# Moving VectorE's length chain between the row maxima in a six-attention stack, with masks and tests on GpSimd

## Chip, cores and metric

The kernel runs on one core of one Trainium2 chip. The metric is the device time of one execution in microseconds. TensorE is called PE here, ScalarE ACT, VectorE DVE, GpSimd POOL and SyncE SP, as in the profile.

## What is computed

A batch of 32 items, each 128 tokens by 256 features in f32, goes through six attentions of 16 heads one after the other. Five have heads of 16 features ("narrow"), the fifth (attention 4) has heads of 64 ("wide"). Two feed-forwards stand behind attentions 1 and 3, and each of the eight parts ends in a residual sum and a layer norm. Cut to what matters here:

```python
mask0 = 1.0 - all(x == 0)                      # per token; mask1 the same on x1
def _mha(x, kv, Wq, Wk, Wv, m, causal):        # attentions 0 and 1
    Q, K, V = (x @ Wq) * m, (kv @ Wk) * m, (kv @ Wv) * m
    energy = Q @ K.T
    lengths = sum(energy[:, :, 0, :] != 0)     # per head, from query row 0
    energy = where(cols >= lengths or (causal and cols > row), -inf, energy)
    return softmax(energy / sqrt(dk)) @ V * m
def mha(q, kv, ...):                           # attentions 2 to 5
    Q, K, V = q @ wq + bq, kv @ wk + bk, kv @ wv + bv
    return softmax(mask(Q @ K.T / sqrt(dk))) @ V @ wo + bo
x = layer_norm(x + attention) * g + b
```

A softmax row sums to 1, so a bias on V adds `bv @ wo` to every output row.

## The kernel before

All weights stay in SBUF. The 32 items go in four rounds of eight. A round has six stages, one for each attention, and a stage has eight slots, one for each item: slot `n` has attention `att(n)` and item `batch(n)` (lines 99 to 112), so there are 192 slots. Stages are called 0 to 5 after their attention; the first two, which find a length, are 0 and 1.

The work of one item is spread over some five slots. Each step has an offset in slots in the table `NARROW` (line 115) or `BROAD` (line 118). `make_orders` (line 125) adds the offset to the slot's number, and sorts. What comes out is one fixed list of steps for each engine, and each engine walks down its list: a step that waits holds up everything behind it on that engine. A step on PE that fills a PSUM tile (`tile`, line 132) has its reader, on ACT or DVE, 0.03 of a slot later. `AFTER_SCORES` is the distance between a score step on PE and the two things read from scores, `max` on DVE and `exp` on ACT.

The steps of a narrow item, in its own order: `XT` (transpose x), `K` and `Q` (projections; ACT evicts K and Q, GpSimd's `keys` expands K), `L` (product of query row 0 with the keys, for the length; GpSimd's `q0` prepares the query), `V`, the score step S, `MT` (the negated row maxima turned by PE, and folded by DVE into Q), the turned score step T, `exp`, `PV` (probabilities times V), `E1` (turned back; DVE divides), and for attentions 2 to 5 `E2` and `E3` (output projection); then `LN` and `LN end`. A feed-forward adds `XT`, `F1`, `F2` and a norm.

Scores have two PSUM buffers, SC0 and SC1, for the halves h = 0 and 1 of the heads. One PE step `ST` does S of one item and T of the item before the last at the same time, in different buffers. There are two of them in a slot: the first writes S into SC0 and T into SC1, the second S into SC1 and T into SC0. So before S is written, the `exp` that reads the T written there last must be done (`free_scores`, lines 510 to 518):

```python
                before = BANK_BEFORE[(part, u)]
                if before[0] == "S":
                    pe.wait_ge(maxima, done("max", before[1]))
                else:
                    pe.wait_ge(probs, done("exp", before[1]))
```

`MT` waits for the second maximum of its slot (line 708). Small tiles go round in a ring of four (`TILES`, line 46), and each waits until the fourth before it has been read. `L` on DVE (lines 1043 to 1067) is a chain of seven instructions, each waiting for the one before; it ends in the keys, which the next S needs. The token mask of attention 1's context is made by `token mask` on POOL (line 1213), `SM` on PE (line 620) and a product on DVE (line 1009).

Of the kernel before, what the change touches and what calls it, by code (L numbers as in the profile page):

```python
# [35 lines left out]
P = 128  # L36
# [86 lines left out]


def make_orders():
# [10 lines left out]
    def norm(at, what, n):  # L136
        put("DVE", at, "LN", what, n)
        put("POOL", at + 0.01, "rstd", what, n)
        put("DVE", at + LN_END, "LN end", what, n)

    steps = {}
    for n in range(SLOTS):
# [32 lines left out]
        tile(n + o["V"], "ACT" if a in (0, 1) else "DVE", "V", n, 0)  # L175
# [21 lines left out]
        if a == 0:  # L197
            put("DVE", n + o["LN"] + LN_END + 0.01, "seen1", b)
# [21 lines left out]
ON_TILES = {"XT", "CT", "SM", "K", "Q", "V", "L", "MT", "PV", "PVW", "E1", "E2", "E3", "F1", "F2", "TP"}  # L220
# [17 lines left out]
def score_bank_users():  # L238
# [32 lines left out]
    "norm_end": [it[1:] for it in pick("DVE", {"LN end"})],  # L271
    "add": [it[1:] for it in pick("POOL", {"add"})],
# [7 lines left out]
assert INDEX["norm"] == INDEX["rstd"] == INDEX["norm_end"] and INDEX["length"] == INDEX["q0"]  # L280
# [41 lines left out]
def build(nc, x, ctx_in, mask_ss, mask_bs, weights, col_bias, row_vec, consts, out):  # L322
    with ExitStack() as stack:
# [6 lines left out]
        def sem(name):  # L330
# [23 lines left out]
        O, OnT, Y, xc = ring(1, "O", [P, D]), ring(1, "OnT", [P, D]), ring(1, "Y", [P, D]), ring(2, "xc", [P, D])  # L354
# [86 lines left out]
        def _(sp):  # L441
# [31 lines left out]
            for kind, b in ORDER["SP"]:  # L473
# [4 lines left out]
                elif kind == "c" and b >= 2:  # L478
                    sp.wait_ge(tile_full, done("tile", ("CT", b - 2)))
# [6 lines left out]
                elif kind == "store":  # L486
                    sp.wait_ge(normed, done("norm", ("att", slot(b, 5))))
# [6 lines left out]
        def _(pe):  # L494
# [109 lines left out]
            for it in ORDER["PE"]:  # L604
# [3 lines left out]
                if kind == "XT":  # L608
# [302 lines left out]
        def _(dve):  # L911
# [58 lines left out]
            for it in ORDER["DVE"]:  # L970
# [344 lines left out]
```

## Time and profile before

| | |
|---|---|
| three runs, median (lowest to highest) | 2756.04 us (2753.00 to 2758.52) |
| the profiled execution, its own time | 2755.75 us |
| its span in the profile | 2753.6 us |
| mean granted clock of TensorE | 0.952 of full speed |
| busy: PE, PE weight loads | 2519.1 us (91%), 2094.6 us (76%) |
| busy: DVE, ACT, POOL | 1600.2 us (58%), 1376.2 us (50%), 827.1 us (30%) |
| chain that ended last, by engine | PE 72%, DVE 11%, issue 7%, POOL 5%, ACT 4% |

The span is the time between the first and the last instruction; the execution's own time has 2.2 us more around it. A busy share is a mean over stages that differ, so the slots have to be looked at stage by stage. The start of each `MT` on PE, one for each narrow slot, is used below to mark slots.

### The profile page before, as it was taken

The page shows a single profiled execution, that of the slowest core. Times are in us where ns is not written, and L with a number is a line of the kernel's source. Part 1 is how long each engine was busy: PE and PEld are TensorE (multiplying, and loading weights), DVE is VectorE, ACT ScalarE, POOL GpSimd, SP SyncE. Part 2 cuts the span into 40 slices and gives each one's busy share as a digit, 9 for nine tenths or more (in the row PEclk, how much of TensorE's full clock was granted, in tenths as well). Part 3 has the DMA queues.
Part 4 walks back from the last instruction along what each step waited for, and adds up shares of the span by engine and source line. Part 5 has one row for each costly group of instructions (what it writes and reads, how often), then busy time and mean ns, then how long its engine had stood idle before and what let it go on. Part 6 is the DMA issues. An engine that isn't in the chain of part 4 may idle for free.

```text
span 2753.6 us, 70667 instructions
## 1 busy us (share of the span) xinstructions
PE 2519.1 (91%) x28737; PEld 2094.6 (76%) x28737; DVE 1600.2 (58%) x3528; ACT 1376.2 (50%) x3364; POOL 827.1 (30%) x1412
## 2 busy tenths in 40 slices
PE   6879999999887999999988899999998889999998
PEld 5667887887766788787766688888786668888876
DVE  4677753445766775344576676544466676644446
ACT  2344565554444456555544456555454445655544
POOL 1234322223233432222323343222232344312222
PEclk8889999999998999999999899999999889999999
DMA  7000000000100000000000000000000000000000
GB/s 245 7 2 2 2 2 1 1 1 10 36 6 2 2 2 2 1 1 2 21 26 4 2 2 2 2 1 1 1 27 23 2 2 2 2 1 1 1 1 17
DMA packets 23778, 32.28 MB, mean 12 GB/s; under 512 B 2305, under 2 KB 22177, under 8 KB 23329
## 3 DMA queue, kind: packets, MB, share of 16 engines
q1 hardware_dynamic: 23456, 27.78, 3.1%
q8 instruction: 229, 3.75, 0.6%
q14 instruction: 93, 0.75, 0.1%
HBM read 23.57 MB, written 4.19 MB: 10 GB/s over the span
## 4 chain that ended last, share of the span: by engine, by line
PE 72%; DVE 11%; issue 7%; POOL 5%; ACT 4%; POOLq 0%; DMA 0%; DVEq 0%; SPq 0%; ACTq 0%
PE M L522 40%; PE SC L685 12%; PE M L528 7%; PE M L721 4%; DVE nmax L1084 3%; POOL Kx L1202 3%; PE M L738 2%; PE SC L584 2%; PE SC L703 2%; PE SC L559 2%; ACT Pr L862 2%; DVE Kx L1063 1%; POOL Y L1228 1%; DVE stats L1151 1%; DVE len_row L1057 1%
## 5 line engine op out<-in xcount | busy, mean ns | idle before, releaser
L1234 POOL TENSOR_TENSOR rstd<-rstd,half 128x1 f32<-128x1 f32 x256 | 184.5, 721 | 1202.6 <-DVE rstd L1155 1201.7
L522 PE MATMUL M<-XT,W 128*128 128x128 f32 x4096 | 540.8, 287 | 2.5 <-ACT H L904 1.5
L522 PEld LDWEIGHTS M<-XT,W 128*128 128x128 f32 x4096 | 519.0, 203 | 20.0 <-issue 2.7
L1084 DVE TENSOR_REDUCE nmax<-SC 128x8 f32<-128x1024 f32 x320 | 389.6, 1217 | 92.0 <-PE SC L685 92.0
L1202 POOL TENSOR_SCALAR Kx<-K,own,k_ones 128x128 f32<-128x128 f32 x640 | 279.6, 451 | 498.7 <-ACT K L815 357.1
L685 PEld LDWEIGHTS SC<-Kx,Qx 32*128 32x128 f32 x5120 | 341.6, 200 | 91.9 <-issue 87.7
L685 PE MATMUL SC<-Qx,Kx 32*128 32x128 f32 x5120 | 398.4, 297 | 0.9 <-DVE Qx L1023 0.9
L685 PE MATMUL SC<-Kx,Qx 32*128 32x128 f32 x5120 | 394.7, 296 | 1.5 <-DVE nmax L1084 1.5
L685 PEld LDWEIGHTS SC<-Qx,Kx 32*128 32x128 f32 x5120 | 333.8, 198 | 3.3 <-issue 1.3
L871 ACT ACTIVATE Pr<-SC 128x1024 f32<-128x1024 f32 x256 | 261.6, 1022 | 69.7 <-PE SC L584 44.3
L841 ACT ACTIVATE Qx<-M,q_bias,q_scale 128x128 f32<-128x128 f32 x640 | 241.8, 474 | 23.4 <-PE M L522 23.4
L862 ACT ACTIVATE Pr<-SC,nmax_w 128x128 f32<-128x128 f32 x512 | 139.0, 383 | 183.3 <-DVE nmax_w L1087 158.1
L1128 DVE TENSOR_TENSOR Y<-M,X 128x256 f32<-128x256 f32 x128 | 54.1, 423 | 271.2 <-PE M L522 271.2
L522 PE MATMUL M<-CT,W 128*128 128x128 f32 x1536 | 207.5, 286 | 0.0
L522 PEld LDWEIGHTS M<-CT,W 128*128 128x128 f32 x1536 | 189.0, 197 | 14.7 <-issue 7.6
L815 ACT ACTIVATE K<-M 128x256 f32<-128x256 f32 x64 | 24.5, 383 | 336.5 <-PE M L522 336.5
L522 PE MATMUL M<-W,CT 128*128 128x512 f32 (+1 forms) x512 | 191.6, 497 | 0.0
L818 ACT ACTIVATE K<-M,CB 128x128 f32<-128x128 f32 x192 | 60.2, 366 | 260.8 <-PE M L522 260.8
L721 PE MATMUL M<-Pr,V 128*32 128x128 f32 x5120 | 173.8, 277 | 0.0
L1252 POOL TENSOR_TENSOR Pr<-Pr,wrec 128x1024 f32<-128x1024 f32 x64 | 121.3, 1895 | 156.7 <-DVE wrec L1099 156.7
L528 PE MATMUL M<-ident,nmax 128*128 128x128 f32 x160 | 48.4, 302 | 130.0 <-DVE nmax L1084 129.9
L798 ACT ACTIVATE XT<-M 128x256 f32<-128x256 f32 x256 | 97.8, 390 | 137.3 <-PE M L528 137.2
(127 smaller groups left out, 4460.3 us busy)
## 6 DMA issues: line engine op xcount, KB each, us to landing
X<-x SPq DMA_DIRECT2D x32, 128.0 KB, 2.1
c_in<-ctx_in SPq DMA_DIRECT2D x32, 128.0 KB, 2.1
out<-X SPq DMA_DIRECT2D x32, 128.0 KB, 1.7
RV<-row_vec SPq DMA_DIRECT2D x1, 2304.0 KB, 12.1
W<-w_k SPq DMA_DIRECT2D x5, 256.0 KB, 9.0
W<-w_q SPq DMA_DIRECT2D x5, 256.0 KB, 12.1
W<-w_v SPq DMA_DIRECT2D x5, 256.0 KB, 7.8
W<-w_f SPq DMA_DIRECT2D x1, 1024.0 KB, 8.9
```

The source lines that it names most:

```text
L522: last = pe.matmul(dst, a, b, start=(k == 0), stop=(k == len(lhsTs) - 1))
L528: last = pe.transpose(dst[:, i * P:(i + 1) * P], src[:, i * P:(i + 1) * P], ident[:, :])
L685: filled[at] = pe.matmul(dst, lhsT, rhs, start=(starting and i == 0), stop=(i == len(line) - 1), skip_group_check=True)
L721: last = pe.matmul(tile_of(it)[32 * t:32 * t + 32, b * P:(b + 1) * P], on_ring(V16, "narrow", n)[:, 4 * b + t, :], p[:, at:at + P], start= ...
L798: act.activation(XT[i % len(XT)][:, :], tile_of(it)[:, 0:D], ACT.Copy).then_inc(tile_act, 1)
L841: last = act.activation(q[:, half_of, c * P:(c + 1) * P], tile_of(it)[:, c * P:(c + 1) * P], ACT.Identity, bias=q_bias[:, which, c, half_o ...
L862: last = act.activation(p[:, i * P:(i + 1) * P], SC[u % 2][:, i * P:(i + 1) * P], ACT.Exp, bias=nm[:, i:i + 1])
L871: last = act.activation(p[:, :], SC[u % 2][:, :], ACT.Exp)
L1084: dve.tensor_reduce(nm, SC[h][:, :].rearrange("p (g c t) -> p g c t", c=KC, t=P), AX_X, ALU.max, negate=True).then_inc(maxima, 1)
L1202: last = pool.tensor_scalar(kx[:, half_of, c * P:(c + 1) * P], k[:, c * P:(c + 1) * P], own[:, half_of:half_of + 1], k_ones[:, half_of, c: ...
L1234: pool.tensor_tensor(r[:, :], r[:, :], half[:, :], ALU.pow).then_inc(rstd_done, 1)
L1252: pool.tensor_tensor(p, p, on_ring(wrec, "wide", u)[:, :].unsqueeze(2).to_broadcast([P, HU, P]), ALU.mult).then_inc(wide_norm, 1)
```

## The change

The steps of the narrow slots get other offsets. `L` moves up on all engines, on DVE to between the two maxima, and the norm `LN` goes behind the second. `AFTER_SCORES` grows from 0.12 to 0.19, for `max` and `exp` alike, in all narrow stages. ACT makes a small column of the first query (`q_col`) before it evicts Q, so that `q0` on POOL need not wait for Q. `L` loses one instruction. The two tests for empty rows go to POOL, only their maxima stay on DVE. The context's mask becomes a product on POOL in place (`context`), a second transpose on PE (`CM`) and an eviction on ACT; `SM` is gone. V's biases are folded once into the rows of the output biases (`VT`, `VB`, in slots 9 to 12 of the first round); V is then only copied, in attention 2 by ACT instead of DVE. The sum `Y` and the statistics `mv` have two buffers instead of one. `by_pool` returns False always, so the branches for a norm on ACT and POOL emit nothing.

```diff
-NARROW = dict(XT=-1.20, SM=-1.25, K=-0.92, Q=-0.86, L=-0.42, V=0.30, CT=0.40, MT=0.86, PV=2.66, E1=3.20, E2=3.54,
-              E3=3.74, XF=4.40, F1=4.62, F2={1: 4.90, 3: 5.10},
-              seen0=-1.15, keys=-0.88, q0=-0.78, mask_row=-0.30, residual=3.30, LN=3.40, SF=0.14)
+NARROW = dict(XT=-1.14, CM=-1.10, CT=-1.92, K=-0.94, Q=-0.88, L=-0.64, V=0.28, MT=0.93, PV=2.62, E1=3.20, E2=3.54,
+              E3=3.72, XF=4.24, F1=4.40, F2={1: 4.66, 3: 4.95}, seen0=-1.0, context=-1.75, keys=-0.80, q0=-0.86,
+              mask_row=-0.30, residual=3.32, LN=3.84)
...
+V_BIAS_AT = {2: 9.32, 3: 10.32, 4: 11.32, 5: 12.32}
 S_STEP, T_STEP = (0.0, 0.5), (1.5, 2.0)
-AFTER_PE, AFTER_SCORES = 0.03, 0.12
-LN_END = 0.25
+AFTER_PE, AFTER_SCORES = 0.03, 0.19
+LN_END = 0.22
...
+def by_pool(norm):
+    return False
...
-        tile(n + o["V"], "ACT" if a in (0, 1) else "DVE", "V", n, 0)
+        tile(n + o["V"], "ACT" if a in (0, 1, 2) else "DVE", "V", n, 0)
...
+                elif kind == "CM":
+                    b = it[1]
+                    pe.wait_ge(cm_done, done("batch", b))
+                    turn(tile_of(it), c_in[b % 2], KC).then_inc(tile_full, 1)
...
+                    if a in MASKED_BY_LENGTH:
+
+                        i = AT["q0"][n]
+                        if i >= 2:
+                            act.wait_ge(q0_done, i - 1)
+                        act.activation(q_col[i % 2][:, :], chunks(tile_of(it)[:, 0:D])[:, :, 0], ACT.Copy,
+                                       scale=DK ** -0.5).then_inc(q_first, 1)
...
-                    dve.tensor_tensor(on_ring(V16, "narrow", n)[:, :, 0:DK],
-                                      tile_of(it)[:, 0:D].rearrange("p (h d) -> p h d", d=DK),
-                                      row(f"v{att(n)}").rearrange("p (h d) -> p h d", d=DK),
-                                      ALU.add).then_inc(tile_dve, 1)
+                    dve.tensor_copy(on_ring(V16, "narrow", n)[:, :, 0:DK],
+                                    tile_of(it)[:, 0:D].rearrange("p (h d) -> p h d", d=DK)).then_inc(tile_dve, 1)
...
+                    dve.tensor_tensor(r, tile_of(it)[:, 0:D], r, ALU.add).then_inc(tile_dve, 1)
...
-                    dve.reciprocal(crec[:, :], cnt[:, :]).then_inc(len_rec, 1)
-                    dve.wait_ge(len_rec, done("length", n))
-
-                    dve.scalar_tensor_tensor(out=lval[:, :], in0=crec[:, :], scalar=-BIG, in1=cnt[:, :], op0=ALU.mult,
-                                             op1=ALU.mult).then_inc(len_val, 1)
+                    dve.reciprocal(lval[:, :], cnt[:, :]).then_inc(len_val, 1)
...
+                    pool.wait_ge(q_first, done("q0", n))
...
+                    pool.tensor_scalar(c_in[b % 2][:, :], c_in[b % 2][:, :], seen1[lane(b)][:, 0:1], None,
+                                       ALU.mult).then_inc(cm_done, 1)
```

**ACT, a slot of stage 5.** `K` and `Qx` are the evictions of K and Q, `Pr<-SC` is an exp, `OnT` evicts E2, `OT` evicts PV. Before, and then with the change:

```order
L818 ACTIVATE K<-M,CB 128x128 x2
L871 ACTIVATE Pr<-SC 128x1024
L841 ACTIVATE Qx<-M,q_bias,q_scale 128x128 x4
L897 ACTIVATE OnT<-M 128x256
L871 ACTIVATE Pr<-SC 128x1024
L885 ACTIVATE OT<-M 128x512
L798 ACTIVATE XT<-M 128x256
```

```order
L869 ACTIVATE K<-M,CB 128x128 x2
L899 ACTIVATE Qx<-M,q_bias,q_scale 128x128 x4
L929 ACTIVATE Pr<-SC 128x1024
L948 ACTIVATE OnT<-M 128x256
L942 ACTIVATE OT<-M 128x512
L929 ACTIVATE Pr<-SC 128x1024
L835 ACTIVATE XT<-M 128x256
```

The first exp has moved from ahead of the eviction of Q to behind it, the second from ahead of the eviction of PV to behind it. The order on PE is the same in this stage. The two moves are in every narrow stage.

**DVE, a slot of stage 0.** `nmax<-SC` is a maximum, `ne` to `Kx` is the length chain, `stats` to `xc` the norm. Both pieces begin with the division behind E1, which follows the first maximum. Before, and then with the change:

```order
L1117 SCALAR_TENSOR_TENSOR O<-M,seen_2,rec 128x256
L1151 BN_STATS stats<-Y 128x6
L1153 BN_AGGR mv<-stats 128x2
L1155 TENSOR_SCALAR rstd<-mv 128x1
L1158 SCALAR_TENSOR_TENSOR xc<-Y,mv,RV 128x256
L1046 TENSOR_SCALAR ne<-M,spare_row 128x128
L1049 TENSOR_REDUCE cnt<-ne 128x1
L1051 RECIPROCAL crec<-cnt 128x1
L1054 SCALAR_TENSOR_TENSOR lval<-crec,cnt 128x1
L1057 TENSOR_SCALAR len_row<-iota,cnt,lval 128x128
L1063 SCALAR_TENSOR_TENSOR Kx<-len_row,spare,Kx 128x256 x2
L1084 TENSOR_REDUCE nmax<-SC 128x4x2
```

```order
L1174 SCALAR_TENSOR_TENSOR O<-M,seen_1,rec 128x256
L1107 TENSOR_SCALAR ne<-M,spare_row 128x128
L1110 TENSOR_REDUCE cnt<-ne 128x1
L1112 RECIPROCAL lval<-cnt 128x1
L1114 TENSOR_SCALAR len_row<-iota,cnt,lval 128x128
L1120 SCALAR_TENSOR_TENSOR Kx<-len_row,spare,Kx 128x256 x2
L1141 TENSOR_REDUCE nmax<-SC 128x4x2
L1207 BN_STATS stats<-Y 128x6
L1216 BN_AGGR mv<-stats 128x2
L1218 TENSOR_SCALAR rstd<-mv 128x1
L1223 SCALAR_TENSOR_TENSOR xc<-Y,mv,RV 128x256
```

The norm no longer stands ahead of the chain and the second maximum; it follows them.

## Rows read from the trace of the kernel before

**Rows 1.** Windows: second round by stage; us, busy (instructions) per engine, clock, DMA
```profile
703.38:802.91 99.53, 83.98 (x1110) 65.58 (x1111) 68.36 (x176) 42.45 (x91) 27.90 (x64) 0.95 0.07 20
802.91:908.53 105.62, 85.73 (x1076) 72.22 (x1077) 70.97 (x171) 42.95 (x92) 39.30 (x80) 0.84 0.01 2
908.53:991.69 83.16, 83.16 (x1134) 66.39 (x1133) 59.40 (x128) 43.68 (x98) 36.04 (x64) 1.00 0.01 2
991.69:1026.67 34.98, 34.98 (x540) 29.26 (x539) 26.06 (x57) 20.86 (x44) 12.58 (x24) 1.00 0.01 3
1026.67:1085.89 59.22, 59.22 (x716) 53.15 (x715) 33.45 (x78) 38.63 (x81) 16.27 (x28) 1.00 0.01 2
...
1328.40:1379.10 50.70, 48.72 (x768) 40.88 (x768) 36.08 (x74) 30.96 (x66) 17.28 (x35) 1.00 0.10 28
```
**Rows 2.** Waits of TensorE: who for whom, us in total, times, longest
```profile
PE M L528 <- DVE nmax L1084: 129.9, 71, 3.5
PE M L625 <- POOL seen_diag L1219: 30.0, 32, 1.5
```
**Rows 3.** Timeline, TensorE then VectorE, one slot of stage 0 (start, us, engine, line)
```profile
764.01 0.30 PE L528 MATMUL M<-ident,nmax 128*128 128x128 f32 x1 [2.30 <-DVE nmax L1084]
764.15 0.59 PE L559 MATMUL SC<-causal_b,ident_b 128*128 128x512 bf16 x2
766.22 1.95 PE L522 MATMUL M<-XT,W 128*128 128x128 f32 x16
775.94 0.39 PE L528 MATMUL M<-ident,nmax 128*128 128x128 f32 x1 [2.35 <-DVE nmax L1084]
...
772.30 0.34 DVE L1046 TENSOR_SCALAR ne<-M,spare_row 128x128 f32<-128x128 f32 x1
774.58 1.21 DVE L1084 TENSOR_REDUCE nmax<-SC 128x8 f32<-128x1024 f32 x1
```
**Rows 4.** Timeline, TensorE then ScalarE, one slot of stage 5
```profile
676.56 0.27 PE L528 MATMUL M<-ident,nmax 128*128 128x128 f32 x1
677.86 1.16 PE L522 MATMUL M<-CT,W 128*128 128x128 f32 x8
678.86 1.06 PE L522 MATMUL M<-XT,W 128*128 128x128 f32 x8
679.75 0.60 PE L528 MATMUL M<-ident,OT 128*128 128x128 f32 x4
681.15 0.38 PE L685 MATMUL SC<-Kx,Qx 32*128 32x128 f32 x2
682.62 1.08 PE L721 MATMUL M<-Pr,V 128*32 128x128 f32 x32
684.82 0.27 PE L528 MATMUL M<-ident,nmax 128*128 128x128 f32 x1
...
679.57 1.02 ACT L871 ACTIVATE Pr<-SC 128x1024 f32<-128x1024 f32 x1
680.48 1.51 ACT L841 ACTIVATE Qx<-M,q_bias,q_scale 128x128 f32<-128x128 f32 x4
683.01 1.02 ACT L871 ACTIVATE Pr<-SC 128x1024 f32<-128x1024 f32 x1
683.91 0.60 ACT L885 ACTIVATE OT<-M 128x512 f32<-128x512 f32 x1
```
**Rows 5.** Timeline of TensorE: two waits and the matmuls behind the first
```profile
644.85 0.33 PE L528 MATMUL M<-ident,nmax 128*128 128x128 f32 x1 [1.45 <-DVE nmax L1084]
646.19 1.99 PE L522 MATMUL M<-CT,W 128*128 128x128 f32 x8
...
703.38 0.30 PE L528 MATMUL M<-ident,nmax 128*128 128x128 f32 x1 [1.39 <-DVE nmax L1084]
```
**Rows 6.** Groups by line: count, busy, mean ns, idle before (ScalarE)
```profile
L798 ACT ACTIVATE XT<-M 128x256 f32<-128x256 f32 x256 | 97.8, 390 | 137.3 <-PE M L528 137.2
L869 ACT ACTIVATE Pr<-SC,key_bias 128x1024 f32<-128x1024 f32 x64 | 71.5, 1117 | 0.1
```

More of the change, by code:

```diff
@@ L138, in norm @@
         put("POOL", at + 0.01, "rstd", what, n)
-        put("DVE", at + LN_END, "LN end", what, n)
+        if by_pool((what, n)):
+            put("ACT", at + 0.12, "normalise", what, n)
+            put("POOL", at + 0.18, "affine", what, n)
+        else:
+            put("DVE", at + LN_END, "LN end", what, n)
     steps = {}
@@ L164, in make_orders @@
         if a == 0:
-            put("DVE", n + o["seen0"], "seen0", b)
+            put("DVE", n + o["seen0"], "largest0", b)
+            put("POOL", n + o["seen0"] + 0.08, "seen0", b)
+        if a == 1:
             tile(n + o["CT"], "ACT", "CT", b)
-        if a == 1:
-            put("POOL", n + o["SM"] - 0.20, "token mask", n)
-            tile(n + o["SM"], "DVE", "SM", n)
+            put("POOL", n + o["context"], "context", b)
+            tile(n + o["CM"], "ACT", "CM", b)
         if a == 3:
@@ L208, in make_orders @@
         put("PE", at, "ST", parts.get("S"), parts.get("T"))
+    for a, at in V_BIAS_AT.items():
+        if a == WIDE:
+            put("DVE", at, "v bias wide", a)
+        else:
+            tile(at, "DVE", "VT", a)
+        tile(at + 0.40, "DVE", "VB", a)
     for b in range(BATCH):
@@ L271 @@
     "norm_end": [it[1:] for it in pick("DVE", {"LN end"})],
+    "affine": [it[1:] for it in pick("POOL", {"affine"})],
     "add": [it[1:] for it in pick("POOL", {"add"})],
@@ L279 @@
 BANK_BEFORE = score_bank_users()
-assert INDEX["norm"] == INDEX["rstd"] == INDEX["norm_end"] and INDEX["length"] == INDEX["q0"]
+assert INDEX["norm"] == INDEX["rstd"] and INDEX["norm_end"] == [key for key in INDEX["norm"] if not by_pool(key)]
+assert INDEX["affine"] == [it[1:] for it in pick("ACT", {"normalise"})] and INDEX["length"] == INDEX["q0"]
 assert INDEX["narrow"] == INDEX["keys"] == INDEX["e1"]
@@ L613, in _ @@
                         what, a = XT_AFTER[j]
-                        pe.wait_ge(normed, done("norm", (what, slot(b, a))))
+                        if by_pool((what, slot(b, a))):
+                            pe.wait_ge(normed_pool, done("affine", (what, slot(b, a))))
+                        else:
+                            pe.wait_ge(normed, done("norm_end", (what, slot(b, a))))
                     turn(tile_of(it), X[lane(b)], KC).then_inc(tile_full, 1)
@@ L883, in _ @@
                         act.wait_ge(tile_full, done("tile", ("E1", before[1]) if before[0] == "PV" else ("E3", before[1] // 2)))
-                    if kind == "PV":
-                        last = act.activation(o[:, :], tile_of(it)[:, :], ACT.Copy)
-                    else:
-                        for t in range(4):
-                            last = act.activation(o[:, t * P:(t + 1) * P], tile_of(it)[:, t * P:(t + 1) * P],
-                                                  ACT.Identity, bias=bias("v4", 4 * (it[1] % 2) + t))
-                    last.then_inc(tile_act, 1)
+                    act.activation(o[:, :], tile_of(it)[:, :], ACT.Copy).then_inc(tile_act, 1)
                 elif kind == "E2":
@@ L967, in _, with free_sum @@
             dve.wait_ge(masks_turned, 1)
+            dve.tensor_scalar(iota[:, :], iota[:, :], -1.0 / BIG, None, ALU.mult)
             dve.tensor_copy(key_bias[:, :], M[TILES - 1][:, 0:BATCH]).then_inc(ready_dve, 1)
+            def free_sum(key):
+                i = AT["norm"][key]
+                if i >= len(Y):
+                    before = INDEX["norm"][i - len(Y)]
+                    if by_pool(before):
+                        once(normalised, done("affine", before))
+                    else:
+                        once(centred, done("norm_end", before))
             for it in ORDER["DVE"]:
```

182 lines of the change are left out of this document (120 added, 62 removed).

## Prediction

> **What bounds the kernel now.** I began with the busy shares: TensorE 91%, nothing else over 58%. That is a mean, so the second view is the round cut by stages [rows 1]. The second round's stages 0 and 1 take 99.53 and 105.62 us with PE busy 83.98 and 85.73; in stages 2 and 3 PE is busy for the whole of 83.16 + 34.98 + 59.22 us, and in the last row, six slots of stage 5, for 48.72 of 50.70. So there are two regimes. Where a length is found, PE waits; elsewhere it is full, and only less PE work or a new wait can change the time. The third view is who PE waits for [rows 2]: 129.9 us for the row maxima, 30.0 us for the token mask.
>
> The timeline of one slot of stage 0 shows why [rows 3]. MT starts at 764.01 and again at 775.94, a slot of 11.93 us, and the second MT waited 2.35. The chain ahead of it is VectorE's: the length chain from 772.30 to the maximum at 774.58 (2.28), then the maximum, 1.21. The scores for that maximum were ready long before; it stood behind norm and chain in VectorE's list. In stage 1 the mask's wait comes on top. The granted clock there is 0.84, in stage 0 it is 0.95, elsewhere 1.00 [rows 1]: waiting makes PE slow as well.
>
> Now the full regime [rows 4]. In stage 5 a slot is 684.82 - 676.56 = 8.26 us with no wait. ACT does exp at 679.57, then evicts Q (680.48 to 681.99); PE writes the second score step at 681.15, just 0.56 after that exp ended at 680.59. The second exp ends at 684.03, PV's eviction follows it. The score buffers are thus freed barely in time. Keep this in view.
>
> **The change, part by part.**
>
> *What VectorE gains in stages 0 and 1.* The chain starts after E1 instead of after the norm. It also loses one small instruction, and two tests go to POOL, which is idle 70% of the span. The maximum then finds both its scores and an idle engine: it no longer sets MT, except where a feed-forward's F2, now just ahead of the second maximum in VectorE's list, holds it.
>
> *What ACT's new order costs in every narrow slot.* The first exp now stands behind Q's eviction, the second behind PV's. PE may not write S before that exp has read the old T. I lay the rows end to end for stage 5, from the first score step at 0. Score step 1.10 (676.76, by its offset behind MT, to 677.86). K and Q on PE 2.06 (677.86 to the end of Q at 679.92), so 3.16. Hop to ACT 0.05, eviction of Q 1.51: 4.72. Exp 1.02, less 0.10 by which ACT's instructions overlap: 5.64. Hop back 0.15 (VectorE's maximum ends at 775.79, MT starts at 775.94 [rows 3]): 5.79. PE would have been there at 4.39, the distance from 676.76 to 681.15: a wait of 1.4. Second step 1.10, O's transposes 0.37 (PV starts at 682.62, which is 1.47 after the step), PV 1.08: 8.34. Hop 0.05, eviction of PV 0.60, exp 0.92, hop 0.15: 10.06. **The slot becomes 10.06 us instead of 8.26.** Six slots of it a round: +10.8 us.
>
> *Stage 2* has mask matmuls in its steps, 2.07 each (764.15 to 766.22 [rows 3]), and K and Q 1.95. The same sum gives 11.9 us. Four of its eight slots also carry stage 1's feed-forward. There x's transpose is evicted behind that exp too (0.39 [rows 6]) and F1 stands ahead of the score step; F2 stands ahead of the maximum. The sum with 0.95 for F1 and for F2 (half of the 16 matmuls of [rows 3]) and 0.5 for F2's sum on VectorE (an estimate: under half of a maximum, which reads four times its columns) is 13.15, 13.15, 14.1 and 14.45. Total 47.6 + 54.9 = 102.5 against 83.16: +19.3.
>
> *Stage 3*: its exp takes 1.12 [rows 6], and each step has a row mask more, an estimated 0.1; hence 10.5, with 1 us more in the first two for stage 2's last masks: 43.4 against 34.98 [rows 1], +8.4. Its four last slots carry the large feed-forward, and PE has enough of its own to cover the exps, but F1 waits for the transpose behind the exp: reached at 4.9, free at 6.2, +1.3 each, +5.2.
>
> *Stage 0* by the same chain: 2.07 + 1.95 + 0.05 + q_col 0.25 + 1.50 + 0.92 + 0.15 + 2.07 + 1.08 + 0.05 + 0.60 + 0.92 + 0.15 = 11.76, against 11.93 at full clock today. So the freed maximum is worth almost nothing: the exps take its place as what PE waits for. Six such slots and two of 11.2: 93.0. q_col is not in the trace. It lies between 0 and the 0.39 of a whole 256-column eviction [rows 6]; I take 0.25, since its two columns leave only the fixed part. The Trainium skill (ScalarE: Activation LUTs, "What ACT_TABLE_LOAD costs") states 186 ns plus 0.833 ns a column for an ACTIVATE with immediate operands. By it q_col is 0.19, and the whole sum 3 us lower.
>
> *Stage 1*: two slots of 11.05, two of 10.1, and four with F1 and F2, 12.7 each, where F1 waits for the transpose and MT for F2 and the maximum: 93.0.
>
> *The rest.* V's bias prelude: four small products and sums once, in slots full of waits, +4 us. CM and CT: four transposes for one small matmul, in the slots above. PVW's evictions become one instead of four, and V is copied instead of added: both off PE's path. The wide stage keeps its own table; I take it as unchanged.
>
> **Sum.** Per round at full clock: +10.8 + 19.3 + 8.4 + 5.2 = +43.7 in the full stages. Stages 0 and 1 go from 205.15 to 186.0, -19.1. Net +24.6, in four rounds +98, with the prelude +102: 2858.
>
> *The clock.* Half speed holds for twice the missing share of the clock: 10 us in stage 0 and 34 in stage 1 [rows 1]. At PE's share of 0.83 this cost 44 x 0.5 x 0.83 = 18 us a round, and the 186.0 above has none of it. The waits get shorter (1.2 to 1.4 instead of 1.85 to 2.36) but there are two a slot. What a wait of this size does, the trace answers both ways [rows 5]: behind 1.45 at 644.85 eight matmuls took 1.99 instead of the 1.16 at 677.86 [rows 4], half speed; behind 1.39 at 703.38 nothing slowed. Bounds 0 and 18; I take half, 9 a round, +36 in all.
>
> The execution profiled took 2755.75, 0.3 under the median of 2756.04, so the sum holds against either: **2894 us**.
>
> **Rivals.**
>
> 1. *The clock does not fall at all* behind waits this short: 2858. For it: four slots with 1.39 and full speed. Against: 644.85.
>
> 2. *The clock falls in every stage that now waits.* The full stages (then 272 us a round) would get stage 0's or stage 1's share of half speed. At 0.95 that is 272 x 0.05 x 0.83 = 11 us a round, at 0.84 it is 36. With 18 in stages 0 and 1: 2858 + 4 x (18 + 11) = 2974, or 3074 at worst. For it: 17% of a slot idle, like stage 0 now; two short waits lie near transposes and 32-row score matmuls. Against: never seen below 1.45. The Trainium skill (TensorE: Matmul & The Clock Gate, "Part 4: PE-mode transpose") says that transposes don't count as work for the clock as other matmuls do. By it this rival's 2974 would be the time, since XT, O and MT stand beside the waits; the slots of 1.39, which have XT right ahead of the wait, speak against it.
>
> 3. *Faster: the exps stay hidden and PE runs full in stages 0 and 1.* Then these 205.15 us shrink to PE's own 169.7 less 18 for the clock, 152: -53 a round, and 2756 - 4 x 53 = 2544. The point that decides is whether Q's eviction plus exp (2.43) fits beside E1 and V on PE (679.75 to 681.15, 1.40). By [rows 4] it does not, in any narrow stage. Smaller gains would need that wait at under a third of my value.
>
> 4. *No change*: the losses of stages 2, 3 and 5 are about 19 a round instead of 43.7. Needs the same.
>
> **How the numbers follow.** Forecast 0.55, rival 1 0.17, rival 2 0.20, rival 3 and smaller gains 0.06, no change 0.02. A measurement of this kernel tells about 0.2% (5.5 us) from nothing. So faster 0.06, same 0.02, slower 0.92. The range: from 2858 down by the bound of q_col and hops that are 0.1 shorter (some 35 us) to 2820, up to rival 2 and a little of its worse half, 2990. That leaves out rivals 3 and 4 and the far end of 2.
>
> **What would show it.** In stages 2, 3 and 5 PE's busy share falls from 100% to about 83%, and PE's waits are for ACT's `Pr`, in two groups, at score steps, some 1.4 and 0.3 us. A slot of stage 5 takes 10.1 us from MT to MT. PE's wait for `nmax` falls from 129.9 to under 40 us, mostly where F2 is; the wait for the token mask is gone. In stage 0 a slot is 11.8, in stage 1's last half 12.7. It is wrong if PE stays at 100% in stage 5, or if stages 0 and 1 fall under 170 us a round.

## The result, and the profile after

The changed kernel takes 2781.31 us (median of 4 runs, 2777.55 to 2785.78) against 2757.28 for the kernel before on the same chip (2753.0 to 2758.53). The ratio is 1.0091, 95% interval 1.0071 to 1.011. So it is slower by 24 us, or 0.9%: little, but clear of the noise. 138 us were forecast, and the time lies under the low end of the range (2820). The profiled execution took 2782.93.

The page of the changed kernel, busy time of TensorE and the chain that ended last:

```profile
PE 2462.5 (89%) x28803; PEld 2019.6 (73%) x28803; DVE 1569.2 (56%) x3346; ACT 1365.4 (49%) x3300; POOL 870.3 (31%) x1476
PE 74%; ACT 16%; issue 5%; DVE 4%; ACTq 0%; POOL 0%; DMA 0%; SPq 0%; POOLq 0%; DVEq 0%
```

PE is *less* busy than before (2519.1 us), though it has slightly more matmuls (28803, before 28737): fewer of them ran slowly, the mean granted clock is 0.990 instead of 0.952. ACT's share of the chain went from 4% to 16%, DVE's from 11% to 4%. Who PE waits for (total, times, longest):

```profile
PE SC L722 <- ACT Pr L929: 69.2, 92, 1.6
PE SC L583 <- ACT Pr L929: 68.8, 87, 1.2
PE M L552 <- DVE nmax L1141: 59.1, 52, 1.6
PE M L546 <- ACT XT L835: 50.6, 45, 1.4
```

The waits for maximum and mask [rows 2] fell from 129.9 to 59.1 and from 30.0 to nothing, and some 138 us of waits for exps took their place. The 50.6 us in the last row are for the transposes that the first product of a feed-forward, F1, reads; their evictions now stand behind an exp on ACT. Now the windows of the second round by stage, cut at the same `MT`s as [rows 1]: 0, 1, 2, first half of 3, second half of 3, the wide stage, stage 5.

```profile
707.62:798.90 91.28, 79.31 (x1102) 59.84 (x1101) 67.71 (x154) 40.67 (x94) 32.67 (x74) 1.00 0.06 18
798.90:890.15 91.25, 75.09 (x1100) 62.65 (x1098) 70.00 (x152) 48.19 (x116) 44.13 (x84) 1.00 0.03 9
890.15:991.62 101.47, 85.30 (x1128) 64.99 (x1129) 53.54 (x123) 45.69 (x104) 36.09 (x64) 1.00 0.01 2
991.62:1033.32 41.70, 35.52 (x540) 29.25 (x539) 26.26 (x57) 21.20 (x45) 12.57 (x24) 1.00 0.01 2
1033.32:1100.39 67.07, 61.93 (x733) 54.55 (x731) 32.95 (x78) 42.16 (x87) 17.14 (x28) 1.00 0.01 2
1100.39:1325.40 225.01, 217.22 (x1762) 183.18 (x1760) 99.82 (x188) 109.28 (x310) 55.55 (x54) 0.98 0.00 1
1325.40:1393.86 68.46, 58.20 (x839) 48.62 (x840) 39.84 (x78) 33.40 (x72) 19.34 (x40) 0.95 0.06 17
```

Stages 0 and 1 gained 8.3 and 14.4 us. Stage 2 lost 18.3, stage 3 lost 6.7 and 7.9. The clock column reads 1.00 in all of them. The wide stage fell from 234.96 to 225.01, which no step of the prediction had. Some 2 us of this are only the mark: the second half of stage 3 now holds 16 more of the products `M<-CT,W` than before (716 matmuls then, 733 now), and the wide stage 16 fewer. Stage 5 lost 10.0, and there the clock reads 0.95 (0.97 before).

The timeline of one slot of stage 5, TensorE and then ScalarE, the counterpart of [rows 4]:

```profile
1354.41 0.27 PE L552 MATMUL M<-ident,nmax 128*128 128x128 f32 x1
...
1360.59 0.38 PE L722 MATMUL SC<-Kx,Qx 32*128 32x128 f32 x2 [1.21 <-ACT Pr L929]
...
1364.26 0.27 PE L552 MATMUL M<-ident,nmax 128*128 128x128 f32 x1
1364.77 0.38 PE L722 MATMUL SC<-Kx,Qx 32*128 32x128 f32 x2 [0.24 <-ACT Pr L929]
...
1358.12 1.50 ACT L899 ACTIVATE Qx<-M,q_bias,q_scale 128x128 f32<-128x128 f32 x4 [0.27 <-PE M L546]
1359.50 1.03 ACT L929 ACTIVATE Pr<-SC 128x1024 f32<-128x1024 f32 x1
1363.21 0.60 ACT L942 ACTIVATE OT<-M 128x512 f32<-128x512 f32 x1 [0.66 <-PE M L758]
1363.70 1.02 ACT L929 ACTIVATE Pr<-SC 128x1024 f32<-128x1024 f32 x1
```

This is the picture that the prediction drew: the exp starts as Q's eviction ends (1359.50), ends at 1360.53, and PE writes scores at 1360.59 after 1.21 us of waiting; the second exp costs 0.24. The slot is 9.85 us (forecast 10.06, before 8.26).

### The profile page after: what moved, and what is told of

It is laid out like the page before. It is cut to its first block, busy times and chain, and to the rows that moved or that the text cites. A ratio compares the mean times of both kernels' runs of the same rounds, so it can differ in the third digit from the quotient of the medians.

```text
span 2781.1 us, 70879 instructions
## 1 busy us (share of the span) xinstructions
PE 2462.5 (89%) x28803; PEld 2019.6 (73%) x28803; DVE 1569.2 (56%) x3346; ACT 1365.4 (49%) x3300; POOL 870.3 (31%) x1476
## 4 chain that ended last, share of the span: by engine, by line
PE 74%; ACT 16%; issue 5%; DVE 4%; ACTq 0%; POOL 0%; DMA 0%; SPq 0%; POOLq 0%; DVEq 0%
PE M L546 40%; PE SC L722 14%; ACT Pr L929 7%; PE M L552 6%; ACT Qx L899 6%; PE M L758 6%; PE SC L583 3%; PE SC L608 2%; PE M L775 2%; PE SC L740 2%; DVE nmax L1141 2%; ACT Pr L927 1%; ACT Pr L920 1%; ACT XT L835 1%; DVE nmax_w L1144 1%
## 5 line engine op out<-in xcount | busy, mean ns | idle before, releaser
L546 PE MATMUL M<-XT,W 128*128 128x128 f32 x4096 | 523.5, 280 | 50.6 <-ACT XT L835 50.6
L546 PEld LDWEIGHTS M<-XT,W 128*128 128x128 f32 x4096 | 495.4, 195 | 76.1 <-ACT XT L835 56.9
L722 PEld LDWEIGHTS SC<-Kx,Qx 32*128 32x128 f32 x5120 | 320.9, 189 | 141.9 <-ACT Pr L929 77.3
L722 PE MATMUL SC<-Kx,Qx 32*128 32x128 f32 x5120 | 370.5, 283 | 58.6 <-ACT Pr L929 57.5
L722 PE MATMUL SC<-Qx,Kx 32*128 32x128 f32 x5120 | 372.1, 283 | 0.9 <-DVE Qx L1087 0.9
L722 PEld LDWEIGHTS SC<-Qx,Kx 32*128 32x128 f32 x5120 | 311.1, 186 | 3.1 <-ACT Pr L929 1.1
L942 ACT ACTIVATE OT<-M 128x512 f32<-128x512 f32 x224 | 134.3, 599 | 315.9 <-PE M L758 215.7
L758 PEld LDWEIGHTS M<-Pr,V 128*32 128x32 f32 x5120 | 130.0, 109 | 33.2 <-issue 27.9
L546 PE MATMUL M<-W,H 128*128 128x256 f32 x640 | 152.0, 384 | 0.0
```

The costliest lines, as they stand in the source:

```text
L546: last = pe.matmul(dst, a, b, start=(k == 0), stop=(k == len(lhsTs) - 1))
L722: filled[at] = pe.matmul(dst, lhsT, rhs, start=(starting and i == 0), stop=(i == len(line) - 1), skip_group_check=True)
L758: last = pe.matmul(tile_of(it)[32 * t:32 * t + 32, b * P:(b + 1) * P], on_ring(V16, "narrow", n)[:, 4 * b + t, :], p[:, at:at + P], start= ...
L942: act.activation(o[:, :], tile_of(it)[:, :], ACT.Copy).then_inc(tile_act, 1)
```

## The experiments

All times are whole-kernel medians, taken on several chips, on which the kernel before took 2754.7 to 2760.0; ratios are against the kernel before, run on the same chip beside them. The table has the second round by stage in us, from `MT` to `MT` in the timelines.

| kernel | 0 | 1 | 2 | 3, first | 3, second | wide | 5 | time | ratio (95%) |
|---|---|---|---|---|---|---|---|---|---|
| before | 99.5 | 105.6 | 83.2 | 35.0 | 59.2 | 234.9 | 58.5 | 2757 | 1 |
| changed | 91.3 | 91.3 | 101.5 | 41.7 | 67.1 | 225.0 | 68.5 | 2781.3 | 1.0091 (1.0071 to 1.011) |
| e1, exps early | 82.0 | 88.0 | 93.2 | 35.0 | 68.1 | 224.0 | 58.8 | 2637.8 | 0.9551 (0.9535 to 0.9568) |
| e2, before with exps late | 108.6 | 98.7 | 96.5 | 41.7 | 68.8 | 227.7 | 68.9 | 2899.7 | 1.0494 (1.0473 to 1.0516) |
| e3, old FF places | 91.3 | 83.8 | 95.6 | 41.7 | 78.9 | 225.1 | 66.9 | 2778.3 | 1.0058 (1.0043 to 1.0073) |
| e4, PVW in four | 91.3 | 91.2 | 101.5 | 41.7 | 67.1 | 225.1 | 68.5 | 2783.4 | 1.0083 (1.0066 to 1.01) |
| e5, e1 with F1, F2 later | 81.9 | 83.6 | 84.8 | 35.0 | 66.7 | 221.9 | 57.2 | 2582.1 | 0.9375 (0.9358 to 0.9393) |
| e6, first exp early | 86.3 | 88.3 | 94.4 | 36.4 | 65.9 | 225.1 | 61.0 | 2668.0 | 0.9686 (0.9669 to 0.9702) |
| e7, e1 with old chain | 112.0 | 120.7 | 93.2 | 35.0 | 68.0 | 222.9 | 58.4 | 2889.8 | 1.0489 (1.0474 to 1.0505) |
| e8, e1 with F2 later | 81.9 | 83.6 | 87.1 | 35.0 | 68.0 | 224.2 | 55.6 | 2598.5 | 0.9426 (0.9408 to 0.9444) |
| e9, e7 with early maxima | 108.6 | 115.1 | 87.1 | 35.0 | 68.0 | 221.3 | 58.3 | 2827.2 | 1.0262 (1.0245 to 1.028) |
| e10, before with new chain | 89.4 | 84.0 | 83.2 | 35.0 | 59.2 | 235.8 | 56.8 | 2623.9 | 0.9525 (0.9511 to 0.9539) |
| e11, e1 with old FF places | 81.9 | 81.3 | 82.3 | 35.0 | 63.7 | 224.2 | 57.2 | 2556.5 | 0.9282 (0.9266 to 0.9297) |
| e12, e10 with PV at 2.62 | 89.4 | 84.0 | 83.2 | 35.0 | 59.2 | 226.6 | 60.1 | 2596.5 | 0.9428 (0.9412 to 0.9445) |

**The exps alone, both ways.** e1 puts only the exps back; e2 moves only the exps in the kernel before.

```diff
 # e1, in the changed kernel
-            put("ACT", n + T_STEP[h] + AFTER_SCORES, "exp", u)
+            put("ACT", n + T_STEP[h] + 0.12, "exp", u)
 # e2, in the kernel before
-            put("ACT", n + T_STEP[h] + AFTER_SCORES, "exp", u)
+            put("ACT", n + T_STEP[h] + 0.20, "exp", u)
```

> The changed kernel with one number undone: the exps of the narrow attentions stand 0.12 of a slot behind their scores on ACT again (ahead of Q's and PV's evictions), the maxima stay at 0.19. Theory (the late exps are the whole loss; the moved length chain is a gain): stages 2, 3 and 5 get back the 43 us a round that they lost, and stages 0 and 1 lose their waits for Pr too, some 10 us a round more: 2781 - 4 x 53 = 2570 us, at least under 2625. Rival (exps early delay q_col and with it the length chain, so that the maximum is late again in stages 0 and 1, +10 us a round or more there): 2640 to 2680. Rival (the loss is from another edit, such as the feed-forward's new place): about 2780.

> The kernel before with that one move alone: the exps 0.20 of a slot behind the scores on ACT, behind Q's and PV's evictions; all else as before. Theory: +40 us a round in stages 2, 3 and 5 and little in 0 and 1, whose slots are set by VectorE there: 2757 + 160 = 2917 us, more if the two waits add up in stages 0 and 1. Rival (exps are hidden, other edits cost the time): 2757 to 2770.

Measured: 143.5 us gained by e1 against the changed kernel, 139.7 lost by e2 against the kernel before on the same chip (2760.0). The move costs nearly the same from either side, and so it does in three places: about 9 us in stage 0, 7 in the first half of 3 and 10 in stage 5. Elsewhere the two differ (8 and 13 us in stage 2, -1 and +10 in the second half of 3, 1 and -7 in the wide stage, 3 and -7 in stage 1), so that the totals agree so well is partly chance. In e1 the narrow exps are gone from PE's waits; in e2 they stand there with 84.3, 73.1 and 49.4 us, beside 136.8 for the maximum that e2 left in place. In stage 1 e2 even got shorter (105.6 to 98.7): PE was busy for 75.8 us there instead of 85.7 with the same matmuls, at a clock of 0.95 instead of 0.84, and its wait for the token mask fell from 6.9 us to 0.2. Why the clock held better is open.

**Which exp.** e6 moves only the first back.

```diff
-            put("ACT", n + T_STEP[h] + AFTER_SCORES, "exp", u)
+            put("ACT", n + T_STEP[h] + (AFTER_SCORES, 0.12)[h], "exp", u)
```

> The changed kernel with only the first exp of a slot (half 0, behind the first score step) put back ahead of Q's eviction; the second stays behind PV's. By the rows laid end to end, a slot of stage 5 is then 7.1 + 0.05 + 0.60 + 0.92 + 0.15 = 8.8 us, against 8.26 with both early and 9.85 with both late; stage 0 is 10.75. Theory (each exp has its own wait, Q's eviction the dearer): some 11 us a round more than with both early: 2680 us. Rival (one late exp is enough to lose it all): 2750 to 2781.

2668.0: the exp behind Q's eviction costs 113 us, the one behind PV's the other 30. Of the 143.5 these are 79% and 21%; of the waits in a slot of stage 5, 1.21 and 0.24, they would be 83% and 17%. The second exp alone late was tried, the first alone late was not.

**Feed-forward places.** e3 undoes them in the changed kernel, e8 and e5 move part of them in e1, e11 undoes them all in e1.

```diff
-              E3=3.72, XF=4.24, F1=4.40, F2={1: 4.66, 3: 4.95}, ...
+              E3=3.72, XF=4.40, F1=4.62, F2={1: 4.90, 3: 5.10}, ...   (e3 and e11)
+              E3=3.72, XF=4.24, F1=4.40, F2={1: 4.72, 3: 4.95}, ...   (e8)
+              E3=3.72, XF=4.24, F1=4.52, F2={1: 4.72, 3: 4.95}, ...   (e5)
```

> The changed kernel with the feed-forwards' old offsets (XF 4.40, F1 4.62, F2 4.90 and 5.10). The wide stage took 235 us a round before and takes 225 now. Theory A (the gain there is F1's eviction, which now stands ahead of the wide exp instead of behind it): it returns to about 235, while the feed-forward slots of stages 1 to 3 lose their waits for F1's transpose and for F2, some 3 + 5 + 5 us: 2775 to 2790 us. Theory B (the gain comes from PVW's single eviction): the wide stage stays at 225, and the total falls to 2730 or so.

> e1_exp_early with F2 of attention 1 at 4.72 alone, so that on VectorE it follows the second maximum. Theory (MT waits 1.4 to 1.5 us in eight slots a round because the maximum stands behind F2): 2638 - 4 x 10 = 2598 us. Rival (the wait only moves, PE has to wait at MT or F2 anyway): 2630 to 2638.

> e1_exp_early with the feed-forwards moved: F1 at 4.52, behind the second score step, so that it no longer stands ahead of it waiting for the transpose, and F2 of attention 1 at 4.72, behind the second maximum on VectorE. Theory (F1's wait for the transpose and the maximum behind F2 cost stages 1 and 2 some 12 us a round, stage 3 some 5 to 8): 2638 - 4 x 18 = 2565 us. Rival (F1's eviction comes too late for the wide stage's transposes and its 4.7 us wait returns): 2590 to 2620.

> The changed kernel with the exps at 0.12 and all feed-forward steps (XF, F1, F2) where they were before. What is left of the change against e10_chain_alone is then the work taken off VectorE (mask as a product on GpSimd, tests on GpSimd, one instruction fewer in the chain), q_col, and V's biases. Theory (these help: e10 still waits 71 us on TensorE for GpSimd's `q0`, which q_col starts a micro-second earlier): 2570 to 2595, some 40 us under e10's 2624, and the waits for `q` fall under 10 us. Rival (they are neutral, and e5_ff_later's 2582 came from its own places of F1 and F2): 2610 to 2640.

With the exps late the places are a draw: e3 gains 13 us a round in stages 1 and 2 and gives 12 back in the second half of stage 3. With the exps early they are a plain loss: e8 gets 39 us back by F2 behind the maximum alone (34 by the ratios), e5 another 14 to 16 by F1, and e11, with all at their old places, takes 2556.5, 81 under e1 and the best kernel here. What a place is worth depends on which wait is open beside it.

e3's second half of stage 3 also shows the clock falling behind a wait. Timeline of TensorE there, a long wait and the matmuls behind it:

```profile
1035.81 0.39 PE L722 MATMUL SC<-mask_row,ones_b 1*128 1x512 bf16 x2 [2.47 <-ACT Pr L927]
1037.02 1.74 PE L546 MATMUL M<-CT,W 128*128 128x128 f32 x8
...
1043.13 1.05 PE L546 MATMUL M<-XT,W 128*128 128x128 f32 x8
```

Eight matmuls take 1.74, half speed, just behind the wait, and 1.05 a few us later. Its window, 1033 to 1112, has a clock of 0.94.

**PVW's eviction**, split in four again in the changed kernel.

```diff
-                    act.activation(o[:, :], tile_of(it)[:, :], ACT.Copy).then_inc(tile_act, 1)
+                    if kind == "PV":
+                        last = act.activation(o[:, :], tile_of(it)[:, :], ACT.Copy)
+                    else:
+                        for t in range(4):
+                            last = act.activation(o[:, t * P:(t + 1) * P], tile_of(it)[:, t * P:(t + 1) * P], ACT.Copy)
+                    last.then_inc(tile_act, 1)
```

> The changed kernel with PVW's eviction in four instructions again (without the bias, which stays folded), so 0.5 us more on ACT, 64 times. Theory A (the wide stage's gain is F1's place): no change within 0.2%, 2781. Theory B (it is PVW's eviction): the wide stage goes back to 235 us a round, 2820.

2783.4 against 2781.3, and no stage moved: nothing, so this is not where the wide stage's 10 us came from. The trace names another place. The timeline of TensorE and then ScalarE in the wide stage of the kernel before:

```profile
1114.68 1.12 PE L528 MATMUL M<-ident,Pr 128*128 128x128 f32 x4 [4.75 <-ACT H L904]
...
1112.20 1.28 ACT L904 ACT_TABLE_LOAD   x1
1113.49 2.17 ACT L904 ACTIVATE H<-M,CB 128x128 f32<-128x128 f32 x8
1115.50 0.65 ACT L885 ACTIVATE OT<-M 128x512 f32<-128x512 f32 x1
```

The same in the changed kernel:

```profile
1124.14 0.65 PE L552 MATMUL M<-ident,Pr 128*128 128x128 f32 x4 [1.13 <-ACT OT L942]
...
1111.96 1.28 ACT L955 ACT_TABLE_LOAD   x1
1114.26 1.14 ACT L955 ACTIVATE H<-M,CB 128x128 f32<-128x128 f32 x4 [1.02 <-PE M L546]
...
1116.27 1.14 ACT L955 ACTIVATE H<-M,CB 128x128 f32<-128x128 f32 x4 [0.59 <-PE M L546]
```

And the window of 20 us at this place, of the kernel before and then of the changed one:

```profile
1110.00:1130.00 20.00, 15.32 (x105) 12.84 (x106) 6.00 (x11) 12.71 (x37) 2.58 (x2) 0.83 0.00 1
```

```profile
1110.00:1130.00 20.00, 18.87 (x179) 16.59 (x178) 8.22 (x16) 13.23 (x34) 6.03 (x5) 1.00 0.00 1
```

Before, PE stood 4.75 us behind one table load and eight evictions of the large feed-forward in a row, and ran slowly behind that (clock 0.83 in this window). After, the load is over before PE's product comes, and the evictions stand in two pieces of four. e10 (below), which has the old table but for chain and norm, still has the 4.75; e11, with the *old* feed-forward places, has 1.05. So it is not F1's place. PV at 2.62 instead of 2.66 was left as a suspect: it puts PV's eviction between the two pieces. e12 tried it alone, in e10.

```diff
-... V=0.30, CT=0.40, MT=0.86, PV=2.66, ...
+... V=0.30, CT=0.40, MT=0.86, PV=2.62, ...
```

> The kernel of e10_chain_alone with the offset of PV at 2.62 instead of 2.66, as the change has it. On ScalarE this puts PV's eviction between the two halves of the eviction of the large feed-forward's H instead of behind both. Theory (this small shift is where the wide stage's 10 us a round went, and what the second half of stage 3 pays 4 us for): the wait of 4.75 us behind H in the wide stage goes, that stage takes 224 to 227 us instead of 235.8, stage 3's second half 63 to 65 instead of 59.2, and the time is 2590 to 2610 against e10's 2624. Rival (other offsets of the change do it): the wait of 4.75 stays, the wide stage takes over 233, and the time is 2620 or more.

The time fell from 2623.9 to 2596.5, the wide stage from 235.8 to 226.6, and TensorE's wait at that place is:

```profile
1034.72 0.66 PE L528 MATMUL M<-ident,Pr 128*128 128x128 f32 x4 [1.05 <-ACT H L904]
```

One offset of 0.04 is worth 27 us here. (In this round stage 5 gave 3.3 of it back, at a clock of 0.94 where e10 had 1.00.) It is not the only way to lose that wait: in e2, with PV at 2.66, the longest wait for `H` is 0.6 us too. The expected price in the second half of stage 3 wasn't there (59.2 in both), so e11's 63.7 has another cause. 2.0 of its 4.4 us are the 16 products that there stand ahead of the mark; the other 2.4 are three waits for `nmax` at score steps (0.59, 0.59 and 1.26), which the maxima at 0.19 would explain; not tried alone.

**The chain.** e7 puts chain and norm back in e1; e9 puts e7's maxima back too; e10 moves only chain and norm in the kernel before.

```diff
 # e7, in e1
-... L=-0.64, ... LN=3.84
+... L=-0.42, ... LN=3.40
 # e9, in e7
-            put("DVE", n + S_STEP[h] + AFTER_SCORES, "max", u)
+            put("DVE", n + S_STEP[h] + 0.12, "max", u)
 # e10, in the kernel before
-... L=-0.42, ... LN=3.40
+... L=-0.64, ... LN=3.84
```

> e1_exp_early with the length chain and the norm of attentions 0 and 1 at their old places (L -0.42, LN 3.40), everything else as in e1. Theory (the chain's new place is what stages 0 and 1 gained): stage 0 back towards 97 and stage 1 towards 100 us from 82 and 88, so 2638 + 4 x 27 = 2745 us. Rival (the gain came from the work taken off VectorE and the mask's wait, the place is worth little): 2640 to 2670.

> The kernel of e7_chain_old (exps early, norm and chain ahead of the second maximum as before), with the maxima at 0.12 again too. In e7 the maximum stood at 0.69 of a slot, and so behind `LN end` (0.65) and stage 0's `largest1` (0.67) on VectorE; before it stood at 0.62, ahead of both. Theory (these pieces in front of the maximum made the overshoot of e7): the waits of 3.9 us for `nmax` fall back to the 2.3 of the kernel before, a slot of stage 0 to 11.9 or less, and the time comes to about 2740 (e1's 2638, plus the 26 us a round that the chain's old place cost in stages 0 and 1 of the kernel before against e1). Rival (GpSimd's order, with `q0` behind ScalarE's q_col and the residual sum behind the keys, makes norm and chain late): the time stays over 2850, with waits for `nmax` over 3 us.

> The kernel before with one part of the change alone: the length chain at -0.64 (between the two maxima) and the norm of stages 0 and 1 at 3.84 (behind the second). The exps, the maxima (0.12), the masks, the tests, V's biases and the feed-forwards stay as before. Theory (the chain's place is what makes e1 fast, the masks and tests off VectorE are small beside it): waits for `nmax` fall from 129.9 to under 70, the token mask's 30 stay, stages 0 and 1 take 172 to 182 us a round together against 205.2, and the time is 2640 to 2670. Rival (the tests, the mask and the freed column of queries do most of it, since the chain's inputs are late without them): over 2700.

e7 took 2889.8, far over what was expected. VectorE in one slot of e7's stage 0, and how PE waits for it:

```profile
794.17 0.48 DVE L1231 SCALAR_TENSOR_TENSOR X<-xc,rstd,RV 128x256 f32<-128x256 f32 x1
794.68 0.42 DVE L1049 TENSOR_REDUCE absmax<-X 128x1 f32<-128x256 f32 x1
795.02 1.22 DVE L1141 TENSOR_REDUCE nmax<-SC 128x8 f32<-128x1024 f32 x1
...
796.38 0.45 PE L552 MATMUL M<-ident,nmax 128*128 128x128 f32 x1 [3.89 <-DVE nmax L1141]
796.62 1.06 PE L583 MATMUL SC<-causal_b,ident_b 128*128 128x512 bf16 x2
```

With the maximum at 0.69, the norm's end and `largest1` stand ahead of it, at 0.62 and 0.64 with the changed kernel's `LN_END` (0.65 and 0.67 are the kernel before's). That is 0.85 us that were behind it before; and 1.06 for two mask matmuls (0.59 at [rows 3]) is half speed. e9 gets the maximum back in front of `largest1` (it now ties with the norm's end, which still goes first) and takes 63 us off, but is still 72 over the kernel before, so neither theory had it alone. GpSimd and VectorE in a slot at the end of e9's stage 0:

```profile
806.67 0.62 POOL L1254 TENSOR_SCALAR q<-q_rows,q_col 128x8 f32<-128x8 f32 x2 [4.64 <-ACT q_col L895]
807.26 1.73 POOL L1266 TENSOR_SCALAR Kx<-K,own,k_ones 128x128 f32<-128x128 f32 x4
808.97 0.93 POOL L1293 TENSOR_SCALAR c_in<-c_in,seen 128x256 f32<-128x256 f32 x1
809.87 0.73 POOL L1306 TENSOR_TENSOR Y<-O,X 128x256 f32<-128x256 f32 x1
...
810.63 0.43 DVE L1207 BATCH_NORM_STATS2 stats<-Y 128x6 f32<-128x256 f32 x1 [3.38 <-POOL Y L1306]
```

VectorE had waited 3.38 us for the residual sum `Y`, which stood behind `q0`, keys and the new context product on GpSimd. That delays norm, chain and maximum, one after the other in this order. The context product is 0.93 of it and stands only in the last two slots of this stage. The slot before has none, and is still 14.4 us long. Its ScalarE, GpSimd and VectorE:

```profile
790.58 0.38 ACT L866 ACTIVATE K<-M 128x256 f32<-128x256 f32 x1 [7.67 <-PE M L546]
791.76 0.18 ACT L895 ACTIVATE q_col<-M 128x2 f32<-128x2 f32 x1
792.64 1.73 POOL L1266 TENSOR_SCALAR Kx<-K,own,k_ones 128x128 f32<-128x128 f32 x4
795.09 0.43 DVE L1207 BATCH_NORM_STATS2 stats<-Y 128x6 f32<-128x256 f32 x1 [2.41 <-POOL Y L1306]
```

And the kernel before, in the slot of [rows 3]:

```profile
767.80 1.73 POOL L1202 TENSOR_SCALAR Kx<-K,own,k_ones 128x128 f32<-128x128 f32 x4 [7.11 <-ACT K L815]
771.16 0.43 DVE L1151 BATCH_NORM_STATS2 stats<-Y 128x6 f32<-128x256 f32 x1 [1.75 <-POOL Y L1228]
```

Before, GpSimd expands the keys as soon as K is evicted. In e9 they stand behind `q0`, and `q0` behind `q_col`, which ScalarE makes after the early exp: K is there at 790.96, the keys start at 792.64. So two new orders on GpSimd, `q0` ahead of the keys and the context product, make the residual sum late, and with the chain in front that costs little, since the norm has time (e11). How much each costs with the old chain place was not tried, nor how much is the slow clock behind the longer waits (0.90 and 0.87 in e9's stages 0 and 1).

e10 is the plainest run: two numbers changed in the kernel before, 2623.9, 132 us faster. Stages 0 and 1 take 173.4 instead of 205.2, at full clock. The wait for the token mask is gone too, though mask and tests are made as before. What PE waits for in those two stages of e10, and then in e11:

```profile
PE M L522 <- POOL q L1189: 16.9, 15, 1.1
PE M L528 <- DVE nmax L1084: 4.2, 4, 1.2
```

```profile
PE M L552 <- DVE nmax L1141: 5.8, 6, 1.4
```

The wait for `q` is what `q_col` was made for: in e10 `q0` must wait for the whole of Q's eviction, in e11 it starts after a column, and 16.9 us a round become nothing. (e11 has two smaller rows more, 2.1 us together.)

**The account.** By steps that each ran: chain and norm moved, -132 (before to e10); PV at 2.62, -27 (e10 to e12); masks, tests, `q_col`, V's biases, PVW's single eviction, the doubled buffers, the other small offsets and the maxima at 0.19 together, -40 (e12 to e11); feed-forwards earlier, +81 (e11 to e1); exps later, +143.5 (e1 to changed). The sum is +25, against 24 measured; it has to agree, since each step starts where the last one ends, and what is over comes from the chips. The sizes hold in this order alone: the earlier feed-forwards cost 81 us with the exps early (e11 to e1) and 3 with the exps late (e3 to changed).

## Why the prediction was wrong in size and right in kind

**Right.** The late exps are what PE waits for, in every narrow stage, with the size given: stage 5's slot 9.85 against 10.06, stage 2's plain slot 11.65 against 11.9, stage 3's 10.25 against 10.5, stage 0's 11.5 against 11.76, the last four slots of stage 1 at 12.3 to 13.0 against 12.7. PE's busy share is 84 to 85% in stage 2, the first half of 3 and stage 5, against about 83%. PE's wait for the mask is gone. Its wait for `nmax` was put at under 40 and is 59.1; that F2 ahead of the maximum makes much of it is shown by e8, where it falls from e1's 73.6 to 35.4. Rival 3, by which the exps stay hidden, did not come about; e1 and e11 show what it would have been worth.

**Wrong, by 111 us against the profiled execution's 2782.93, in four terms:**

1. *The clock, +36 forecast, about 0 measured.* "I take half" of the cost today was a choice between two rows of opposite sign [rows 5]. The windows above have 1.00 in stages 0 to 3, with two waits a slot beside transposes. Rival 1 had this term, though its 2858 is still 75 us too high. The timeline of TensorE in a slot of stage 0, after:

```profile
763.76 0.27 PE L552 MATMUL M<-ident,nmax 128*128 128x128 f32 x1
765.20 0.60 PE L583 MATMUL SC<-causal_b,ident_b 128*128 128x512 bf16 x2 [1.16 <-ACT Pr L929]
771.80 0.60 PE L583 MATMUL SC<-causal_b,ident_b 128*128 128x512 bf16 x2 [0.82 <-ACT Pr L929]
775.26 0.27 PE L552 MATMUL M<-ident,nmax 128*128 128x128 f32 x1
```

The slot idles 1.98 us, nearly as much as the 2.35 of [rows 3], but in two pieces, and the masks behind each take 0.60, full speed. The prediction went by idle time alone, and that did not decide it. In stages 0 to 3 of the second round, where no wait was over 1.5 us the clock reads 1.00 (changed, e1, e10, e11), and where it reads 0.84 to 0.95 there is a wait of 2.3 or more (before, e2, e3, e7, e9). Between them lies the second half of stage 3 in e2, with 1.98 and 1.00. That is a pattern of these runs and no rule. Stage 1 of the kernel before, with the lowest clock of all (0.84), has one such wait, of 3.11; the others come in close pairs such as 0.99 at 813.64 and 1.85 at 816.02. Behind 2.30 at 764.01 the next masks still ran at full speed [rows 3]; behind 1.45 at 644.85, at the end of the wide stage, eight matmuls did not [rows 5]. And the changed kernel's own stage 5 starts slowly, behind 1.45 at 1325.40, with nothing over 1.64 after it:

```profile
1325.40:1345.00 19.60, 16.04 (x191) 13.37 (x191) 8.65 (x13) 7.95 (x18) 4.91 (x10) 0.83 0.01 2
1345.00:1393.86 48.86, 42.16 (x648) 35.25 (x649) 31.19 (x66) 25.45 (x56) 14.43 (x30) 1.00 0.07 23
```

So what makes the clock fall stays open, and that it did not fall in stages 0 to 3 is measured and not explained. Rival 2's 2974, which it also found by the Trainium skill (TensorE: Matmul & The Clock Gate, "Part 4: PE-mode transpose"), did not come about: full speed was held in stages 0 to 3 with transposes beside the waits. Whether transposes count for less is not shown either way.

2. *The wide stage "unchanged" and stage 3's second half "+5.2": +21 forecast, -8 measured.* The second half of stage 3 lost more (7.9 a round; three of its FF products wait 1.44 for the transpose, the forecast had 1.3), but the wide stage gained 10, some 2 of them by the mark and the rest by the wait of 4.75 above, as e12 shows (9.3 with the mark as before). I took a stage as unchanged since its own table was; but it shares ACT with the last narrow items and their feed-forward. [rows 1] leaves this stage out, and so did I: its 235 us were never asked for their waits.

3. *Each slot 0.2 us too long, about -28 in four rounds.* Stages 0, 1, 2, the first half of 3 and stage 5 came out 7.0 us a round under the forecast. I took 0.15 for the way from an exp's end to PE, from VectorE's maximum to `MT` [rows 3]. At a score step it is 0.06 (1360.53 to 1360.59) and 0.05. This does not go by the engine: in the same trace PV's product in the wide stage starts 0.14 us after the ScalarE eviction that it waits for, in all of its 12 waits. `q_col` took 0.17 to 0.19, not 0.25. The Trainium skill (ScalarE: Activation LUTs, "What ACT_TABLE_LOAD costs") gave 0.19 for it, and the trace agrees. One sum of the record does not come out of its own terms: four slots of 10.5 with 1 us more for the first two are 43 or 44 us, and not 43.4; that is 2 us in four rounds at most.

4. *The first round and the ends, about -17*, which is what the other three leave. The prelude's +4 can't be seen: the second round starts only 4.2 us later than before, and the first `MT` comes at 30.65 instead of 34.77.

36 + 29 + 28 + 17 = 110. The first two are the steps that failed: half of today's clock loss was put on waits that cost no clock in stages 0 and 1, and a stage was called unchanged that had a wait of 4.75 us to lose. All four have the same sign, which the range didn't allow for: its low end took the terms' bounds but kept rival 1's 2858 as a floor, with only 35 us under it for hops.

## What to carry to other kernels

Where one double-buffered resource links two engines, the reader that frees it goes ahead of every eviction that only feeds later work; a shared constant for two readers on two engines (`AFTER_SCORES`) hid that one wanted to be late and the other early. Undo a change part by part even if the sum looks like nothing: here +24 us was -199 and +225 (in the order tried), and the best kernel keeps the first alone. Ask a stage that you call unchanged for its longest wait, since an offset moved by 0.04 may remove it.

## What the runs showed of the hardware

- Full clock was held with PE busy for 82% of a stage (75.09 of 91.25 us) where its longest wait was 1.49 us. It was not held where PE was busier: before, stage 0, 84%, with waits of up to 2.36, clock 0.95; changed, stage 5, 85%, with waits of up to 1.64, clock 0.95. e9, with waits up to 4.9, had 0.90 and 0.87 in stages 0 and 1.
- From the end of what TensorE waited for to its next matmul it took 0.05 to 0.06 us at score steps (ScalarE's exp), 0.14 at the wide PV (ScalarE's eviction) and 0.05 to 0.15 at `MT` (VectorE's maximum).
- Between two functions of ScalarE a table load took 1.28 us (1111.96 in the changed kernel).
